# Denominators of a causal attention stage: one column sum per block instead of one per diagonal tile, with the diagonal tiles added on VectorE and the reciprocals taken in a 128x16 tile that travels through DRAM

## The reference

```
xn  = layernorm(x)
q, k, v = xn @ Wq, xn @ Wk, xn @ Wv          # 16 query heads, 4 key/value heads, head size 32
s   = q k^T * 32**-0.5, causal               # each key/value head serves 4 query heads
att = softmax(s) @ v                         # 2048 x 2048 scores per head
out = x + att @ Wo + moe(xn)                 # 32 experts, 6 per token, and a shared expert
```

## Time and profile before

| what | value |
| --- | --- |
| median of 3 runs | 3957.03 us (3955.51 to 3959.78) |
| profiled execution, its own time | 3962.08 us |
| its span | 3960.3 us |
| TensorE (PE) busy | 3643.3 us, 92% |
| VectorE (DVE) busy | 2354.1 us, 59% |
| ScalarE (ACT) busy | 1631.7 us, 41% |
| GpSimd (POOL) busy | 2080.3 us, 53% |
| granted TensorE clock, mean | 0.959 of 2.4 GHz |

### The profile page before, as it was taken

How to read it: one execution, slowest core, us unless ns; L and a number is a source line. 1 busy time by engine, 2 the same in 40 slices (tenths; PEclk the granted TensorE clock), 3 DMA queues, 4 the chain that set the end, 5 groups by cost and what they waited for, 6 DMA issues and landing times. The chain is left out here.

```text
span 3960.3 us, 56437 instructions
## 1 busy us (share of the span) xinstructions
PE 3643.3 (92%) x19856; PEld 2255.2 (57%) x19856; DVE 2354.1 (59%) x5384; ACT 1631.7 (41%) x3341; POOL 2080.3 (53%) x1604
## 2 busy tenths in 40 slices
PE   7888988898888799999999999999999999999789
PEld 5666766676666555555545455545555554554267
DVE  5334443354433344487778777877787777875134
ACT  3122221222211111165556565656565655655511
POOL 1322233222233222277787777877787778778800
PEclk9889988899998899999999999999999999999989
DMA  5222322232221499801221122112210221020086
GB/s 161 72 90 74 109 84 72 74 104 87 93 72 61 134 301 302 237 16 47 52 49 30 33 52 49 32 32 52 51 40 22 52 52 39 22 55 7 10 294 225
DMA packets 228172, 340.55 MB, mean 86 GB/s; under 512 B 65088, under 2 KB 75968, under 8 KB 227968
## 3 DMA queue, kind: packets, MB, share of 16 engines
q1 hardware_dynamic: 197232, 307.77, 25.4%
q0 software_dynamic: 17920, 12.82, 1.6%
q10 hardware_dynamic: 12816, 17.33, 1.2%
HBM read 217.15 MB, written 120.35 MB: 85 GB/s over the span
## 5 line engine op out<-in xcount | busy, mean ns | idle before, releaser
L1337 ACT ACTIVATE prb<-sps 128x512 f32<-128x512 f32 (+3 forms) x2560 | 1187.9, 539 | 782.1 <-PE sps L1435 748.7
L1360 DVE TENSOR_REDUCE mx<-mps 128x1 f32<-128x512 f32 x1440 | 939.6, 681 | 174.5 <-PE mps L1417 174.4
L1281 POOL TENSOR_TENSOR rows<-rows,prb 128x1024 f32<-128x1024 f32 x384 | 905.7, 2387 | 0.0
L390 POOL DMA_INDIRECT tab_s<-pay,slot x384 | 377.7, 983 | 976.6 <-DVE tokf L674 856.4
L1449 PE MATMUL ops<-prb,vst 128*32 128x512 f32 (+3 forms) x5120 | 599.8, 540 | 29.4 <-POOL prb L1267 28.9
L1363 DVE CUSTOM_DVE_ANT_0 mps<-mps,bias 128x256 f32<-128x256 f32 (+1 forms) x960 | 489.5, 523 | 223.4 <-PE mps L1417 223.2
L1276 POOL TENSOR_TENSOR rows<-prb 128x1024 f32<-128x1024 f32 x192 | 454.0, 2386 | 165.5 <-ACT prb L1337 165.5
L1417 PE MATMUL mps<-x_lo,w_lo 96*128 96x512 f32 (+2 forms) x1280 | 487.6, 387 | 8.7 <-DVE mx L1360 3.3
L1435 PE MATMUL sps<-w_lo,x_lo 97*128 97x512 f32 (+2 forms) x1280 | 476.8, 393 | 17.1 <-ACT prb L1337 17.1
L1435 PE MATMUL sps<-w_hi,x_hi 97*128 97x512 f32 (+2 forms) x1280 | 483.3, 389 | 9.8 <-ACT prb L1337 8.0
L730 PE MATMUL acc<-x_hi,w_hi 128*128 128x512 f32 x1088 | 434.9, 400 | 12.0 <-DVE qk_lo L576 8.0
(11 more groups left out here) (169 smaller groups left out, 4285.2 us busy)
## 6 DMA issues: line engine op xcount, KB each, us to landing
wgu<-in_e_gu SPq DMA_DIRECT2D x24, 1408.0 KB, 6.6
rows<-in_x SPq DMA_DIRECT2D x16, 1024.0 KB
xn_s<-rows SPq DMA_DIRECT2D x16, 1024.0 KB, 5.1
y_sb<-in_x SPq DMA_DIRECT2D x16, 1024.0 KB
q_hi_s<-qk_hi SPq DMA_DIRECT2D x16, 1024.0 KB, 4.2
q_lo_s<-qk_lo SPq DMA_DIRECT2D x16, 1024.0 KB, 6.6
base<-y_sb SPq DMA_DIRECT2D x16, 1024.0 KB
w_hi<-q_hi_s SPq DMA_DIRECT2D x64, 256.0 KB, 4.4
```

The source lines that it names most:

```text
L390: nc.gpsimd.indirect_dma_start(t["tab"], bass.IndirectOffsetOnAxis(ap=slot[:, i, k:k + 1], axis=0), pay[:, i, k, :], None, bounds_check=E ...
L1281: nc.gpsimd.tensor_tensor(acc4, acc4, prb[:, (2 * (k - 1) + pr) % RP], ALU.add).then_inc(add_done, 1)
L1337: nc.scalar.activation(prb[:, (2 * k + h // 2) % RP, h % 2, q0:CH], sps[:, (GROUP * k + h) % R, q0:CH], ACT.Exp, scale=SCALE).then_inc(exp ...
L1360: V.tensor_reduce(mx[:, h * NKT + qt, j:j + 1], mps[:, n % R, 0:wr], AX.X, ALU.max).then_inc(mred_done, 1)
```

## The change

VectorE adds the r = 1, 2 and 3 tiles of a block's diagonal into a new tile `dsum`, columns 128 to 511, each two steps behind the step that made it. TensorE then sums `dsum` and the first 128 columns of the r = 0 tile once per block (`denominators`, one step after the block's last value product). The copy of `dps` moves from k = last + 3 to k = last + 4. The reciprocal is taken of each denominator once: the SP queue writes one row per head of `den` to DRAM (four transfers), reads them back as a 128x16 tile `dsm`, VectorE inverts it at k = last + 7 into `rsm`, and the SP queue writes that to DRAM and reads it back into `rden`, repeated over each head's 32 rows (four transfers). GpSimd multiplies at k = last + 10 instead of last + 7. Of GpSimd's six adds, the last one of the second pair moves one step later where its step is a diagonal one. The list `work` deals the pieces differently.

```diff
-        work = [1.0 * (CH - max(r, 0) * P) + (1.1 if steps[k - LAG][2] < 0 else 1.6) *
+        work = [1.0 * (CH - max(r, 0) * P) + 1.1 * (CH - max(steps[k - LAG][2], 0) * P) + CH
...
+            def invert(i, p, j):
+                n = (2 * i + p) * JC + j
+                sp.wait_ge(den_done, n + 2)
+                for h in range(GROUP):
+                    sp.dma_start(t["den"][j % 2, h:h + 1], den[j % 2][HD * h:HD * h + 1, :]).then_inc(den_out, 16)
+                sp.wait_ge(den_out, 16 * GROUP * (n + 1))
+                sp.dma_start(dsm[j % 2][:], t["den"][j % 2].rearrange("h (c e) -> (h c) e", e=EL)).then_inc(dsm_in, 16)
+                sp.wait_ge(rsm_done, n + 1)
+                sp.dma_start(t["rec"][j % 2].rearrange("h (c e) -> (h c) e", e=EL), rsm[j % 2][:]).then_inc(rec_out, 16)
+                sp.wait_ge(rec_out, 16 * n + 16)
+                for h in range(GROUP):
+                    sp.dma_start(rden[j % 2][HD * h:HD * (h + 1), :],
+                                 t["rec"][j % 2, h:h + 1].to_broadcast([HD, CH])).then_inc(rden_in, 16)
...
                     for j in range(JC - 1):
+                        invert(i, p, j)
                         store(i, p, j)
...
                     load_v(sp, t, att, i + 1, p)
+                    invert(i, p, JC - 1)
                     store(i, p, JC - 1)
...
-                    if k - LAG - NT - 1 in lasts:
-                        normalize(bg, lasts.index(k - LAG - NT - 1))
+                    if k - SCALED in lasts:
+                        normalize(bg, lasts.index(k - SCALED))
...
+            def add_diagonal(bg, k):
+                for pr in range(2):
+                    dve.wait_ge(sel_done, bg * 2 * len(diag) + 2 * diag.index(k) + pr + 1)
...
+                    V.tensor_tensor(dsum[:, pr, :, q0:CH], so_far, tile, ALU.add).then_inc(dadd_done, 1)
...
+                    if k - INVERTED in lasts:
+                        invert(bg, lasts.index(k - INVERTED))
...
+            def denominators(bg, j):
+                pe.wait_ge(dadd_done, 6 * (bg * JC + j + 1))
+                for h in range(GROUP):
+                    M(dps[HD * h:HD * (h + 1), P:CH], ones[:], dsum[:, h // 2, h % 2, P:CH],
+                      start=(j == 0), stop=False, skip_group_check=True)
+                for h in range(GROUP):
+                    last = M(dps[HD * h:HD * (h + 1), 0:P], ones[:], prb[:, (2 * k + h // 2) % RP, h % 2, 0:P],
+                             start=False, stop=True, skip_group_check=True)
...
-                if r >= 0:
-                    for h in range(GROUP):
-                        last = M(dps[HD * h:HD * (h + 1), q0:CH], ones[:],
-                                 prb[:, (2 * k + h // 2) % RP, h % 2, q0:CH], start=(r == 0 and j <= 1),
-                                 stop=(r == 3), skip_group_check=True)
```

More of the change, by code:

```diff
@@ L1154, in stage_b @@
         ones = sb("ones_b", [P, HD])
+        EL = GROUP * CH // P
+        dsm = two("dsm", [P, EL])
+        rsm = two("rsm", [P, EL])
+        dsum = sb("dsum", [P, 2, 2, CH])
         sps = ps("sps", [P, R, CH])
@@ L1191, in stage_b @@
         M1 = 37
-        work = [1.0 * (CH - max(r, 0) * P) + (1.1 if steps[k - LAG][2] < 0 else 1.6) *
-                (CH - max(steps[k - LAG][2], 0) * P) + CH for k, (j, kt, r) in enumerate(steps)][:M1]
+        work = [1.0 * (CH - max(r, 0) * P) + 1.1 * (CH - max(steps[k - LAG][2], 0) * P) + CH
+                for k, (j, kt, r) in enumerate(steps)][:M1]
         for k in range(M1):
-            if any(k - LAG - 1 - part in lasts for part in range(NT)) or LAG <= k < LAG + NT:
-                work[k] -= 400
+            if k - LAG - 1 in lasts or k == LAG:
+                work[k] += 1.1 * CH
+            for r in (1, 2, 3):
+                if steps[k - LAG][2] == r:
+                    work[k] -= 230 * (NT - r)
+            if k - INVERTED in lasts or k == INVERTED - 1:
+                work[k] -= 100
         cost = [64 + piece[5] for piece in pieces]
@@ L1377, in group @@
             def group(bg, p, nxt, prev=True):
                 for k in range(NK):
-                    if nxt:
-                        for n in quota(k):
-                            reduce(bg + 1, 1 - p, n)
-                        if k == MFIN:
-                            negate(bg + 1)
-                    for part in range(NT):
-                        if k - LAG - 1 - part in lasts:
-                            invert(bg, lasts.index(k - LAG - 1 - part), part)
-                        if prev and k == LAG + part:
-                            invert(bg - 1, JC - 1, part)
+                    todo = list(quota(k)) if nxt else []
@@ new lines, in group @@
+                    for n in todo[:len(todo) // 2]:
+                        reduce(bg + 1, 1 - p, n)
+                    if k >= LAG and steps[k - LAG][2] > 0:
+                        add_diagonal(bg, k - LAG)
+                    if prev and k < LAG:
+                        add_diagonal(bg - 1, NK + k - LAG)
+                    for n in todo[len(todo) // 2:]:
+                        reduce(bg + 1, 1 - p, n)
+                    if nxt and k == MFIN:
+                        negate(bg + 1)
@@ L1389, in group @@
+                    if k - INVERTED in lasts:
+                        invert(bg, lasts.index(k - INVERTED))
+                    if prev and k == INVERTED - 1:
+                        invert(bg - 1, JC - 1)
                 if not nxt:
-                    for part in range(NT):
-                        invert(bg, JC - 1, part)
+                    for k in range(NK - LAG, NK):
+                        add_diagonal(bg, k)
+                    invert(bg, JC - 1)
             group(0, 0, True, prev=False)
@@ L1461, in sum_of_four @@
                 j, kt, _ = steps[fours[gi]]
[L1462 removed]
+                opens = kt == 0
                 if opens:
@@ L1489, in group @@
                         output(bg - 1, 1 - p, NK + k - LAG)
+                    if k - LAG - 1 in lasts:
+                        denominators(bg, lasts.index(k - LAG - 1))
+                    if prev and k == LAG:
+                        denominators(bg - 1, JC - 1)
                     for n in todo[GROUP:]:
@@ L1499, in group @@
                         output(bg, p, k - LAG)
+                    denominators(bg, JC - 1)
             def ready(bg, p):
```

61 lines of the change are left out of this document (43 added, 18 removed).

## The result

The changed kernel takes 4084.0 us (median of 4 runs, 4083.39 to 4089.14), the kernel before 3957.81 us in the runs beside it: a ratio of 1.032, with 1.030 to 1.034 as its 95% interval. It is slower by 126 us. The forecast was 3942, the range ended at 4005, so time and sign are both missed.

What follows compares the result with a forecast made beforehand. The prediction took TensorE to bound stage B, with the other engines having 20% or more to spare on average. Its terms, -106 - 28 + 38 + 73 + 8 = -15 us, gave a median of 3942 us, range 3870 to 4005.

Steps and rivals of the forecast that it cites:

- TensorE's column sums: Stage B, TensorE: one 512-column sum in place of 1280 columns saves 1.65 us a block, -106 us.
- Late triangles: GpSimd's moved tree add takes away most of TensorE's 28.9 us of waiting for late triangles, -28 us.
- VectorE's work: Six adds for four reciprocals a block come in lumps that delay TensorE's pieces, 2.5 us a group, +38 us.
- The way of block 0's reciprocal: VectorE waits about 5.2 us behind step 10 for the DRAM transfers in 14 groups, all reaching TensorE, +73 us.
- What is hidden: The DRAM ways of blocks 1, 2 and 3 are covered by other steps and cost nothing.
- The end of stage B: The last block's reciprocal way has nothing to cover it, 11.1 us in place of 3.5, +8 us.
- GpSimd and VectorE get in each other's way: Rival: VectorE's two-input adds and GpSimd's SBUF reads block each other, 3 us a group, +45 us, 3987 us; chance 0.34.

Runs made afterwards that it cites:

- fourth_only: Kernel before with only the last tree add of the second pair one step later where its step is a diagonal one; ratio 0.993, period 128.38 us.
- one_input: Changed kernel with each VectorE add replaced by a maximum reduction over the same tile, one SBUF input; ratio 1.010, period 132.74 us.
- pool_after_adds: Changed kernel with GpSimd's first tree add of a block's first four steps waiting for all six adds of the block before; ratio 1.015, period 133.43 us.
- early_only: Changed kernel with block 0's denominators sent ahead of block 3's store on the SP queue; ratio 1.034, period 138.64 us.
- one_input_early: Changed kernel with reductions in place of VectorE's adds and block 0's denominators sent ahead of block 3's store; ratio 0.988, period 127.00 us.
- even_list: Changed kernel without VectorE's adds, block 0's denominators sent early, pieces dealt without deductions for adds and reciprocal; ratio 0.990, period 126.43 us.
- no_adds: Changed kernel without VectorE's six adds per block, the column sum reading the r = 1 tile alone; ratio 0.987, period 126.23 us.

## Why the prediction was wrong, by its own steps

Three steps failed: the collisions of VectorE's adds with GpSimd, which the sum put at nothing, cost 11.6 us a group; TensorE's column sums gave back about 32 us and not 106; and the clock had no term. The rest is right or mis-sized by less.

**TensorE's column sums, -106 us.** They measured about -32, with 29 to 41 us by the medians. Two things failed. The price, 1.65 us a block, was taken from a start-to-start distance that held the return to full-width matmuls; it is 1.29, 82 us in all. And "what TensorE no longer does is gained, unless another engine's list then stops it": it stops it, by VectorE's pieces and by the load of the next group's weights.

**Late triangles, -28 us.** Right: `fourth_only` gave -26 us by its ratio (-25 us in the 15 periods).

**VectorE's work, +38 us.** As lumps without collisions, 127.00 - 126.35 = 0.65 us a group, +10 us; by the medians, 47 and 66 us under the kernel before, it is up to +20. The three buffers cover more than I reckoned. The term was mis-sized by some 20 to 30 us, inside its bounds.

**The way of block 0's reciprocal, +73 us.** Place, chain and count were right; the length was not. I gave 3.3 and 2.1 us to the two transfers. They took 2.03 from issue to issue and 1.7, since the four small issues follow each other 0.29 us apart, not 0.45, and the last of them has landed 1.2 us later, not 2.0. In group 7, counted from step 8's exponentials, the store left at 4.1 us (forecast 4.0), `dsm` landed at 9.9 (11.4), and VectorE was ready at 6.7 (6.3). The wait was 3.2 us. Its price beside reductions in place of adds is nevertheless 5.7 us a group, 86 us, because the clock adds up to 3.3 of them; without any such work it is about 1. In the changed kernel it hides behind the collisions and can't be separated.

**What is hidden.** Right: of the 19 waits for `dsm`, 14 are block 0's (3.0 to 3.4 us each) and the other five stand in the last group, where no pieces are left.

**The end of stage B, +8 us.** Measured +5.5: 9.0 us (3877.8 to 3886.78) in place of the 3.5 of the earlier trace rows:

```profile
3877.19 0.60 ACT L1354 ACTIVATE four<-dps 128x512 f32<-128x512 f32 x1 [2.31 <-PE dps L1511]
```

```profile
3886.78 1.26 POOL L1288 TENSOR_TENSOR y_sb<-four,y_sb 128x512 f32<-128x512 f32 x1 [15.19 <-DMA y_sb<-rec_s]
```

**The rival that came true.** *GpSimd and VectorE get in each other's way*, which I gave 0.34 and 3 us a group. The mechanism is shown by `one_input` and `pool_after_adds`, the price is 11.6 us a group (`early_only` less `one_input_early`). Of its three places, block 0's r = 3 add in step 5 was right. For block 2 I named step 23 and it is step 25, block 1's in step 13 I left out, both because the first tree add of the next block starts there. For block 3 I named the r = 3 add, and it is the r = 1 add in step 37. I had looked for the places in nominal steps and not in the order of exponentials and adds. The Trainium skill (SBUF — State Buffer, who interferes with whom) states the rule: two SBUF inputs on VectorE against a GpSimd instruction that reads SBUF, for its whole length. The runs agree: 2.6 us for 0.41, and a reduction of the same size never over 0.955. The hold-up can also last longer than one instruction: block 3's first r = 1 add took 4.2 us in group 7, over a tree add and zeroings on both sides of it. I had worked out 7 us a group from it, and with its 105 us in 15 groups the sum would have been -106 - 28 + 38 + 73 + 8 + 105 = +90 us: the right sign, and some 36 us short of the 126. I weighed it down because no row showed the two kinds at once; there was no row because the kernel before has no such instruction in this stage, which is no evidence against the rule.

**The clock.** No term, in a stage that stood at 1.00. In the changed kernel it is up to 89 of the 126 us. It is hardly a separate cause there: 33 of its 34 stretches at half clock begin in steps 5, 6, 13 and 26, in or right behind TensorE's stops, and in `one_input_early`, with neither collisions nor the wait, 24 us are left (`even_list` has 78, behind stops elsewhere). But the stops cost about as much again behind them: in the 14 periods TensorE stands still for 112 us, 50 before, and the half clock takes up to 89 more.

**The sum again**, in us a group against before: triangles -1.6, columns -2.0, lumps +0.6, gives the 127.0 of `one_input_early`. On top, +11.6 for the collisions with the clock that they bring, and nothing more for block 0's wait: 138.6, measured 138.4. The terms are differences between neighbouring runs, so up to the 138.6 of `early_only` they add up by construction. Only the last step, from there to the changed kernel, tests something.

**What stays open.** Why the wait costs about 1 us a group in `no_adds` and 5.7 with the reductions is argued from the number of pieces behind it, not tried apart. How many collisions a list without any overlap would leave, and whether the whole change would then beat `fourth_only`, wasn't tried.

## What to carry to other kernels

Before work is moved to an engine with a low busy share, look at what the instruction reads: an add of two SBUF tiles on VectorE beside an engine of long SBUF adds waits by whole instructions, and everything in order behind it waits too. Price a matmul from the distance that changes when it is missing, and ask what TensorE waits for next once it is gone. In a stage like this one, at full clock before, a new stop of TensorE cost about twice its length.

## What the runs showed of the hardware

- A VectorE add of 128x256 elements with both inputs in SBUF took up to 2612 ns in place of 409, behind a GpSimd add of 128x1024 (2.4 to 2.5 us); an add of 128x768 took up to 4.9 us, longer than one GpSimd add. A reduction of the same tiles stayed at 403 to 955 ns, a reciprocal of 128x128 at 894 to 954.
- Stops of 1.3 to 3 us of a TensorE that is 94% to 96% busy on average were followed by 1.2 GHz (0.53 and 0.66 granted in the windows above); 184 us of the 15 groups in the changed kernel.
- Small transfers on the SP queue took, by their medians, 1.4 us (a tile of 128x16 to DRAM) and 1.6 us (the same from DRAM) from issue to landing. Four rows of 2 KB, issued 0.29 us apart, had all landed 1.2 us behind the last issue; the 256 KB store took 2.0.
- A set of eight 32-column matmuls of 512 columns took 0.86 us between others of its kind and 0.99 us before a full-width matmul.
